# A transformer layer on one core: the normalised rows of a pair all written by ScalarE, none by VectorE

## Chip, cores and metric

The kernel runs on one core of a Trainium2 chip. The metric is the device time of one execution in microseconds (us). ACT is ScalarE, DVE is VectorE, PE is TensorE (PEld its weight loads), POOL is GpSimd, SP is SyncE.

## Reference

A layer in float32 on x of shape (16, 256, 128): attention with two heads of 64, then a feed-forward part with a routed low-rank term, both between norms.

```python
def _layernorm(x, axis=-1, eps=1e-05):
    m = jnp.mean(x, axis=axis, keepdims=True)
    v = jnp.var(x, axis=axis, keepdims=True)
    return (x - m) / jnp.sqrt(v + eps)
...
    # attention: q, k, v from the normalised rows, half of each head rotated, softmax, Wo
    # ffn: x @ W.T + the low-rank term of the best of 4 experts (ranks 1, 2, 4, 8), weighted
x = L0_attn_x
x = x + _layernorm(_L0_attn_ref(_layernorm(x, axis=-1), ...), axis=-1)
x = x + _layernorm(_L0_ffn_ref(_layernorm(x, axis=-1), ...), axis=-1)
return x
```

The change touches the first `_layernorm`, the one ahead of the attention.

## The kernel before

The 16 batches are taken in 8 pairs. A pair has 512 rows, which lie in SBUF (`x_all`) as four tiles of 128 partitions x 128 columns. Every engine has its own instruction list, written out by hand; inside it nothing is reordered. Engines meet only at semaphores.

All engines run the same loop over passes, `for a in PASSES`, from -1 to 9. Pass a holds the attention of pair a, the projections of pair a+1, the end of the attention and the second norm of pair a-1, the routing and the last residual of pair a-2, and at its end the first norm of pair a+2. Passes -1 to 5 have such a first norm (pairs 1 to 7); that of pair 0 is done ahead of the loop, by `normalise_first` on ACT (L291), four tiles in a row.

The first norm of pair n goes as follows. DVE takes statistics (`stats`, `gap`, `mean`, `variance`); POOL raises the variance to the power -0.5 (`norm_rows`, L201) and makes the shift (`norm_shift`, L206 and L208), which posts `rstd1`. Then the four tiles of `xn` are written as scale x + shift, tiles 0 and 1 by DVE (`normalise` with half 0, a tensor_scalar, L464) and tiles 2 and 3 by ACT (`normalise`, an activation Identity with a scale and a bias per partition, L296). Each tile adds 1 to `xn_ready`. PE waits for all four and transposes them into the bank ps_b:

```python
def turn_x(n):
    pe.wait_ge(xn_ready, 4 * n + 4)
    ...
    for t in range(PT):
        last = pe.transpose(ps_b[:, t * P:(t + 1) * P], xn[:, t, :], ident[:, :])     # L831
```

ACT copies ps_b to `xn_up` (`rows_up`, L301), DVE takes the remainder as `xn_low` (`rows_low`, L469, early in the next pass), and PE multiplies both by the projection weights (L838 to L840).

What stands around it at the end of a pass. On PE: `weigh(a, 2)` (L877 into ps_c), `project_z(a-1, 0)` (L898), `turn_x(a+2)` (L831), `project_z(a-1, 1)` (L898), `scores(a+1, 0)` (L857), `weigh(a, 3)` (L877 into ps_a). On ACT: `x2_copy` (L338), `variance_y` (L332), `qkt_copy` (L316), `normalise` (L296), `probs_copy(a, 3)` (L327), `rows_up` (L301), `v_copy` (L311). On DVE: `variance_2` (L516), `normalise` (L464), four `residual_z` (L599), `weights_sum` (L480), `scaled_bias` (L521), `add_head` (L488), `add_bias(a-1, 0)` (L527), `add_head`; then, in the next pass, `add_bias(a-2, 1)` (L527), which needs the second `project_z`, `rows_low` (L469), two small reductions and `row_max` (L475), which lets ACT go on with the exponentials (`exps`, L321) of the next pair. In passes -1 and 0 several one-off steps of `later_weights` are mixed in (L606 and L607 on DVE, L931 on PE, which waits for L630 on DVE).

Of the kernel before, what the change touches and what calls it, by code (L numbers as in the profile page):

```python
# [21 lines left out]
PT = 2 * TILES  # L22
# [21 lines left out]
def layer(nc, x, w_attn, vectors, w_ffn, w_down, sim, out):  # L44
# [3 lines left out]
    with ctx:  # L48
        def sb(name, shape, dt=F32):
            return ctx.enter_context(nc.sbuf_tensor(name, shape, dt))  # L50
# [4 lines left out]
        def sem(name):  # L55
            return ctx.enter_context(nc.semaphore(name))
# [26 lines left out]
        x_all, y_all = sb("x_all", [P, B * T]), sb("y_all", [P, PAIRS * PT, VW])  # L83
# [3 lines left out]
        ve1, mean1, rs1, nm1 = sb("ve1", [P, 2, PT]), sb("mean1", [P, 2, PT]), sb("rs1", [P, 2, PT]), sb("nm1", [P, 2, PT])  # L87
        xn, xn_up, xn_low = sb("xn", [P, PT, E]), sb("xn_up", [P, PT, P], F32R), sb("xn_low", [P, PT, P], F32R)
# [42 lines left out]
        link1, var1, pool1, rstd1 = sem("link1"), sem("var1"), sem("pool1"), sem("rstd1")  # L131
        xn_ready, xt_done, xt_out, xt_low = sem("xn_ready"), sem("xt_done"), sem("xt_out"), sem("xt_low")
# [15 lines left out]
        def has(n):  # L148
            return 0 <= n < PAIRS

        def rows(n, t):
            return slice(n * PT * E + t * E, n * PT * E + (t + 1) * E)
# [123 lines left out]
        def _(act):  # L276
# [15 lines left out]
                                   bias=nm1[:, 0, t:t + 1], scale=rs1[:, 0, t:t + 1]).then_inc(xn_ready, 1)  # L292

            def normalise(n):
                for t in (2, 3):
                    act.activation(xn[:, t, :], x_all[:, rows(n, t)], ACT.Identity,  # L296
                                   bias=nm1[:, n % 2, t:t + 1], scale=rs1[:, n % 2, t:t + 1]).then_inc(xn_ready, 1)

# [67 lines left out]
            for a in PASSES:  # L366
                now, nxt, done = has(a), has(a + 1), has(a - 2)
# [52 lines left out]
        def _(dve):  # L420
# [35 lines left out]
            def variance(n):  # L456
                dve.wait_ge(link1, n * 3 + 3)
                dve.scalar_tensor_tensor(ve1[:, n % 2, :], tmp1[:, 1, :], 1.0 / E, tmp1[:, 2, :], ALU.mult, ALU.add).then_inc(var1, 1)  # L458

            def normalise(n, half):  # L460
                if half == 0:
                    dve.wait_ge(rstd1, n + 1)
                for t in (2 * half, 2 * half + 1):
                    dve.tensor_scalar(xn[:, t, :], x_all[:, rows(n, t)], rs1[:, n % 2, t:t + 1], nm1[:, n % 2, t:t + 1],  # L464
                                      ALU.mult, ALU.add).then_inc(xn_ready, 1)

            def rows_low(n):
                dve.wait_ge(xt_out, n + 1)
                dve.tensor_tensor(xn_low[:, :, :].rearrange("p t c -> p (t c)"), ps_b[:, :],  # L469
                                  xn_up[:, :, :].rearrange("p t c -> p (t c)").bitcast(F32), ALU.subtract).then_inc(xt_low, 1)  # L470


            def row_max(n, u):
                dve.wait_ge(scores_done, n * 4 + u + 1)
                dve.tensor_reduce(neg_max[:, u, :], ps_s[u % 2][:, :].rearrange("p (j k) -> p j k", j=TILES),  # L475
                                  AX.X, ALU.max, negate=True).then_inc(max_ready, 1)
# [47 lines left out]
            def add_bias(n, k):  # L524
                dve.wait_ge(scaled, n + 1)
                dve.wait_ge(r_done, n * 2 + k + 1)
                dve.tensor_tensor(route[:, 2 * k:2 * k + 2, :], ps_z[k][:, :, 0:RW],  # L527
                                  bias_s[:, 2 * k:2 * k + 2, :], ALU.add).then_inc(route_ready, 1)
# [4 lines left out]
            def top_logit(n):  # L533
                dve.wait_ge(route_ready, n * 2 + 2)
                dve.tensor_reduce(top[:, :], route[:, :, PROJ + RANK:RW], AX.X, ALU.max).then_inc(route_link, 1)

            def square_sum(n):
                dve.wait_ge(squared, n + 1)
                dve.tensor_reduce(norm2[:, :], proj_sq[:, :, :], AX.X, ALU.add).then_inc(route_link, 1)
# [15 lines left out]
            def top_key(n):  # L555
                dve.wait_ge(route_link, n * 10 + 4)
                dve.tensor_reduce(key_top[:, :], key[:, :, :], AX.X, ALU.max).then_inc(route_link, 1)
# [143 lines left out]
            link(dve.tensor_scalar(bias_y[:, :], bias_y[:, :], mean_w[:, 3:4], None, ALU.subtract), fold_link)  # L701

            for a in PASSES:
                now, nxt, far, last_, done = has(a), has(a + 1), has(a + 2), has(a - 1), has(a - 2)
                if done:
                    add_bias(a - 2, 1)
                if nxt and a >= 0:
                    rows_low(a + 1)
                if done:
                    top_logit(a - 2)  # L710
                    square_sum(a - 2)
                if now:
                    row_max(a, 0)
                if done:
                    length(a - 2)
                if last_:
                    weights_sum(a - 1, 3)
                if done:
                    below_top(a - 2)
                if last_:  # L720
                    add_head(a - 1, 3, 0)
                    add_head(a - 1, 3, 1)
                if now:
                    row_max(a, 1)
                if a == 0:
                    later_weights(1)
                if a == 1:
                    later_weights(5)
                if done:
                    keys(a - 2)  # L730
                if has(a + 3):
                    stats(a + 3, 0)
                if done:
                    top_key(a - 2)
                    logits(a - 2)
                    is_top(a - 2)
                if has(a + 3):
                    stats(a + 3, 1)
                    stats(a + 3, 2)
                if done:  # L740
                    shares(a - 2)
                    pick(a - 2)
                if has(a + 3):
                    stats(a + 3, 3)
                if done:
                    sum_exps(a - 2)
                if last_:
                    residual_y(a - 1, 0)
                if done:
                    invert_sum(a - 2)  # L750
                if has(a + 3):
                    gap(a + 3)
                if done:
                    gates(a - 2)
                if has(a + 3):
                    mean(a + 3)
                if done:
                    gates_up(a - 2)
                if has(a + 3):
                    variance(a + 3)  # L760
                if done:
                    gates_low(a - 2)
                if now:
                    row_max(a, 2)
                if last_:
                    residual_y(a - 1, 1)
                    residual_y(a - 1, 2)
                if now:
                    row_max(a, 3)
                    weights_sum(a, 0)  # L770
                if a == 0:
                    later_weights(2)
                if last_:
                    stats_2(a - 1, 0)
                if now:
                    add_head(a, 0, 0)
                if last_:
                    stats_2(a - 1, 1)
                if now:
                    add_head(a, 0, 1)  # L780
                if last_:
                    residual_y(a - 1, 3)
                    stats_2(a - 1, 2)
                    stats_2(a - 1, 3)
                if now:
                    weights_sum(a, 1)
                if last_:
                    gap_2(a - 1)
                if now:
                    add_head(a, 1, 0)  # L790
                if last_:
                    square_2(a - 1)
                if now:
                    add_head(a, 1, 1)
                if last_:
                    variance_2(a - 1)
                if far:
                    normalise(a + 2, 0)
                if done:
                    residual_z(a - 2, 0)  # L800
                    residual_z(a - 2, 1)
                    residual_z(a - 2, 2)
                if done:
                    residual_z(a - 2, 3)
                if now:
                    weights_sum(a, 2)
                if a == -1:
                    later_weights(0)
                if a == 0:
                    later_weights(3)  # L810
                if last_:
                    scaled_bias(a - 1)
                if now:
                    add_head(a, 2, 0)
                if last_:
                    add_bias(a - 1, 0)
                if now:
                    add_head(a, 2, 1)
                if a == 0:
                    later_weights(4)  # L820
# [209 lines left out]
```

## Time and profile before

| what | value |
|---|---|
| time, median of 3 runs | 167.34 us (165.85 to 168.54) |
| time of the profiled execution | 168.68 us |
| its span, first to last instruction | 166.9 us |
| mean granted TensorE clock, as a share of full speed | 0.92 |
| PE busy | 132.7 us, 80% |
| DVE busy | 131.6 us, 79% |
| ACT busy | 112.0 us, 67% |
| POOL busy | 90.6 us, 54% |

The profile records one execution, whose time lies 1.78 us above its span and 1.34 us above the median. An engine's share of busy time is a mean over the start, the steady passes and the end, which have different limits. "Idle before" gives the time in which an engine stood still before an instruction, and the instruction that released it.

### The profile page before, as it was taken

What the parts mean: (1) busy time and instruction counts of PE and PEld (TensorE: products, weight loads), DVE (VectorE), ACT (ScalarE), POOL (GpSimd) and SP (SyncE); (2) the same over time, 40 slices, a digit from 0 to 9 for tenths busy, and PEclk for the clock granted to TensorE, in tenths of its full rate; (3) what the DMA queues carried; (4) which work ended last, traced back from release to release, by engine and by line L of the source; (5) the groups of instructions that cost most, each with busy time, mean ns of one, the idle gap of its engine ahead of it and who ended that gap; (6) DMA issues with size and microseconds to landing.
All of it is one profiled execution on the core that took longest, in us unless ns stands there. A gap on an engine that the chain in (4) does not pass through costs nothing.

```text
span 166.9 us, 3027 instructions
## 1 busy us (share of the span) xinstructions
PE 132.7 (80%) x865; PEld 108.6 (65%) x865; DVE 131.6 (79%) x560; ACT 112.0 (67%) x369; POOL 90.6 (54%) x150
## 2 busy tenths in 40 slices
PE   0468589967998999999999999999999799256030
PEld 0246267855887869887977897797889589145020
DVE  4669947586888899899979998897898889774512
ACT  3167535955979699879969996997998667240130
POOL 6272850670465586849657774976469516405202
PEclk9999957999999999999999999999999999965555
DMA  4533240000000000100010010001001000101001
GB/s 106 174 83 108 68 121 0 6 0 0 2 0 4 2 0 0 67 0 0 2 67 2 0 41 22 4 0 63 2 6 63 0 4 13 50 0 63 2 0 63
DMA packets 4912, 5.02 MB, mean 30 GB/s; under 512 B 369, under 2 KB 4640, under 8 KB 4896
## 3 DMA queue, kind: packets, MB, share of 16 engines
q1 hardware_dynamic: 4512, 4.46, 8.5%
q10 hardware_dynamic: 384, 0.38, 1.0%
q8 instruction: 7, 0.11, 0.3%
q14 instruction: 9, 0.07, 0.2%
HBM read 2.74 MB, written 2.10 MB: 29 GB/s over the span
## 4 chain that ended last, share of the span: by engine, by line
PE 46%; DVE 23%; ACT 18%; POOL 4%; DMA 3%; issue 3%; POOLq 1%; DVEq 0%; ACTq 0%
PE ps_s L857 6%; PE ps_z L898 6%; PE ps_a L877 5%; ACT probs L321 5%; PE ps_b L831 4%; DVE neg_max L475 3%; DMA x_all<-x 3%; PE ps_c L877 3%; ACT sq_y L332 3%; PE ps_a L867 2%; DVE x_all L495 2%; PE ps_z L912 2%; ACT qk_t L316 2%; PE ps_b L877 2%; ACT sq_z L355 2%
## 5 line engine op out<-in xcount | busy, mean ns | idle before, releaser
L321 ACT ACTIVATE probs<-ps_s,neg_max 128x256 f32<-128x256 f32 x64 | 27.1, 486 | 11.8 <-DVE neg_max L475 11.8
L475 DVE TENSOR_REDUCE neg_max<-ps_s 128x2 f32<-128x512 f32 x32 | 21.6, 681 | 4.0 <-PE ps_s L857 4.0
L857 PE MATMUL ps_s<-qk_t 64*128 64x256 f32 x128 | 19.2, 418 | 0.9 <-ACT probs L321 0.9
L877 PE MATMUL ps_a<-v_all,probs_t 128*128 128x129 f32 x128 | 18.0, 283 | 0.0
L217 POOL TENSOR_TENSOR turn<-qk,sin_x 128x256 f32<-128x256 f32 x16 | 11.9, 746 | 9.7 <-ACT qk L305 9.3
L877 PEld LDWEIGHTS ps_a<-v_all,probs_t 128*128 128x128 f32 x128 | 15.6, 191 | 2.3 <-issue 2.3
L228 POOL TENSOR_TENSOR inv_norm<-norm,power 128x4 f32<-128x4 f32 x8 | 8.1, 1015 | 15.0 <-DVE norm L544 15.0
L898 PE MATMUL ps_z<-w_z,x_t 128*128 128x190 f32 x64 | 14.2, 357 | 2.0 <-DVE x_all L599 2.0
L857 PEld LDWEIGHTS ps_s<-qk_t 64*128 64x128 f32 x128 | 11.9, 195 | 5.8 <-issue 5.2
L232 POOL TENSOR_TENSOR rsy<-var_y,power 128x4 f32<-128x4 f32 x8 | 8.6, 1070 | 12.6 <-ACT sq_y L332 12.6
L495 DVE SCALAR_TENSOR_TENSOR x_all<-y_all,rsy,x_all 128x128 f32<-128x128 f32 x32 | 13.7, 448 | 0.8 <-POOL rsy L232 0.8
L599 DVE SCALAR_TENSOR_TENSOR x_all<-ps_z,rsz,x_all 128x128 f32<-128x128 f32 x32 | 9.0, 342 | 6.1 <-POOL rsz L238 6.1
L898 PEld LDWEIGHTS ps_z<-w_z,x_t 128*128 128x128 f32 x64 | 11.2, 208 | 2.5 <-DVE x_all L599 2.4
L220 POOL TENSOR_TENSOR qk<-qk,cos_x 128x256 f32<-128x256 f32 x16 | 12.1, 754 | 1.3
L201 POOL TENSOR_TENSOR rs<-ve,power 128x4 f32<-128x4 f32 x8 | 8.1, 1018 | 8.0 <-DVE ve L458 8.0
L223 POOL TENSOR_TENSOR qk<-qk,turn 128x256 f32<-128x256 f32 x16 | 11.6, 726 | 1.3
L332 ACT ACTIVATE sq_y<-y_all 128x129 f32<-128x129 f32 x32 | 9.9, 325 | 2.6 <-DVE y_all L488 2.6
L242 POOL TENSOR_TENSOR std<-ve,root 128x4 f32<-128x4 f32 x8 | 8.2, 1030 | 5.7 <-DVE ve L516 5.7
L867 PE MATMUL ps_a<-ident,probs 128*128 128x128 f32 x64 | 9.7, 274 | 1.8 <-DVE y_all L488 1.8
L236 POOL TENSOR_TENSOR var_z<-var_z,eps 128x4 f32<-128x4 f32 x8 | 1.6, 204 | 17.3 <-ACT sq_z L355 17.3
L905 PE MATMUL ps_d<-ident_r,gated 128*128 128x128 f32 x8 | 2.5, 308 | 10.0 <-DVE gated L593 10.0
L327 ACT ACTIVATE probs_t<-ps_a 128x512 f32<-128x512 f32 x16 | 9.8, 614 | 0.6 <-PE ps_a L867 0.5
(205 smaller groups left out, 423.8 us busy)
## 6 DMA issues: line engine op xcount, KB each, us to landing
x_all<-x SPq DMA_DIRECT2D x8, 256.0 KB, 2.8
out<-x_all SPq DMA_DIRECT2D x7, 256.0 KB, 2.1
vec<-vectors ACTq DMA_DIRECT2D x1, 273.0 KB, 4.3
w_raw<-w_attn SPq DMA_DIRECT2D x1, 256.0 KB, 5.1
out<-x_all SPq DMA_DIRECT2D x2, 128.0 KB, 1.7
ffn_raw<-w_ffn ACTq DMA_DIRECT2D x1, 71.5 KB
down_raw<-w_down ACTq DMA_DIRECT2D x1, 23.5 KB
sim_raw<-sim ACTq DMA_DIRECT2D x1, 0.5 KB
```

What stands on the lines that cost most here:

```text
L217: pool.tensor_tensor(turn[:, b, :, :, :], swapped, sin_x[:, :, :, :, :].rearrange("p t g h i -> p (t g) h i"), ALU.mult).then_inc(rope_mid, 1)
L220: pool.tensor_tensor(spatial, spatial, cos_x[:, :, :, :, :].rearrange("p t g h i -> p (t g) (h i)"), ALU.mult).then_inc(rope_mid, 1)
L223: pool.tensor_tensor(spatial, spatial, turn[:, b, :, :, :].rearrange("p g h i -> p g (h i)"), ALU.add).then_inc(rope_done, 1)
L321: last = act.activation(probs[:, u, j, :], ps_s[u % 2][:, j * T:(j + 1) * T], ACT.Exp, bias=neg_max[:, u, j:j + 1])
L327: act.activation(probs_t[:, u, :, :], unit_bank[u][:, :].rearrange("p (a t) -> p a t", a=TILES), ACT.Copy).then_inc(pt_out, 1)
L332: last = act.activation(sq_y[:, t, :], y_all[:, n * PT + t, :], ACT.Square, scale=E ** -0.5, accum_out=var_y[:, t:t + 1])
L475: dve.tensor_reduce(neg_max[:, u, :], ps_s[u % 2][:, :].rearrange("p (j k) -> p j k", j=TILES), AX.X, ALU.max, negate=True).then_inc(max_r ...
L495: dve.scalar_tensor_tensor(x_all[:, rows(n, t)], y_all[:, n * PT + t, 0:E], rsy[:, t:t + 1], x_all[:, rows(n, t)], ALU.mult, ALU.add).then ...
L857: last = pe.matmul(ps_s[h][:, j * T:(j + 1) * T], qk_t[r, b, 0, j * P:(j + 1) * P], qk_t[r, b, 1, :], start=True, stop=True)
L867: last = pe.transpose(unit_bank[u][:, i * T + j * P:i * T + (j + 1) * P], probs[:, u, j, i * P:(i + 1) * P], ident[:, :])
L877: last = pe.matmul(unit_bank[u][:, j * VW:(j + 1) * VW], probs_t[:, u, i, j * P:(j + 1) * P], v_all[:, at:at + VW], start=(i == 0), stop=( ...
L898: last = pe.matmul(ps_z[k][:, t, :], x2_t[:, 2 * k + t, :], w_z[:, :], start=(t == 0), stop=False, skip_group_check=True)
```

## The change

In passes -1 to 5 the tiles 0 and 1 of `xn` move from DVE to ACT, so that ACT writes four tiles and DVE none. The count that PE waits for stays the same. The lines behind the removed function move up by 7, those behind the removed call by 9.

```diff
@@ scalar
             def normalise(n):
-                for t in (2, 3):
+                for t in range(PT):
                     act.activation(xn[:, t, :], x_all[:, rows(n, t)], ACT.Identity,
                                    bias=nm1[:, n % 2, t:t + 1], scale=rs1[:, n % 2, t:t + 1]).then_inc(xn_ready, 1)
@@ vector
-            def normalise(n, half):
-                if half == 0:
-                    dve.wait_ge(rstd1, n + 1)
-                for t in (2 * half, 2 * half + 1):
-                    dve.tensor_scalar(xn[:, t, :], x_all[:, rows(n, t)], rs1[:, n % 2, t:t + 1], nm1[:, n % 2, t:t + 1],
-                                      ALU.mult, ALU.add).then_inc(xn_ready, 1)
...
-                now, nxt, far, last_, done = has(a), has(a + 1), has(a + 2), has(a - 1), has(a - 2)
+                now, nxt, last_, done = has(a), has(a + 1), has(a - 1), has(a - 2)
...
-                if far:
-                    normalise(a + 2, 0)
```

On ACT at the end of pass 0, the piece of the difference of its instruction list:

```order
 L332 ACTIVATE sq_y,var_y<-y_all 128x129 x2
 L316 ACTIVATE qk_t<-ps_s 128x512
-L296 ACTIVATE xn<-x_all,nm,rs 128x128 x2
+L296 ACTIVATE xn<-x_all,nm,rs 128x128 x4
 L327 ACTIVATE probs_t<-ps_a 128x512
 L301 ACTIVATE xn_up<-ps_b 128x512
```

Two more activations stand between the copy of qk_t and that of probs_t; passes 1 to 5 read the same, and in pass -1 the four stand directly ahead of L301.

On DVE at the end of a steady pass (here pass 3), the kernel before:

```order
L516 SCALAR_TENSOR_TENSOR ve<-tmp 128x4
L464 TENSOR_SCALAR xn<-x_all,rs,nm 128x128 x2
L599 SCALAR_TENSOR_TENSOR x_all<-ps_z,rsz,x_all 128x128 x4
L480 RECIPROCAL den<-ps_c 128x2
L521 TENSOR_TENSOR bias_s<-bias_b,std 128x248
L488 SCALAR_TENSOR_TENSOR y_all<-ps_c,den,bias_y 128x128
L527 TENSOR_TENSOR route<-ps_z,bias_s 128x124
L488 SCALAR_TENSOR_TENSOR y_all<-ps_c,den,bias_y 128x128
L527 TENSOR_TENSOR route<-ps_z,bias_s 128x124
L469 TENSOR_TENSOR xn_low<-ps_b,xn_up 128x512
```

and the changed kernel at the same place:

```order
L509 SCALAR_TENSOR_TENSOR ve<-tmp 128x4
L592 SCALAR_TENSOR_TENSOR x_all<-ps_z,rsz,x_all 128x128 x4
L473 RECIPROCAL den<-ps_c 128x2
L514 TENSOR_TENSOR bias_s<-bias_b,std 128x248
L481 SCALAR_TENSOR_TENSOR y_all<-ps_c,den,bias_y 128x128
L520 TENSOR_TENSOR route<-ps_z,bias_s 128x124
L481 SCALAR_TENSOR_TENSOR y_all<-ps_c,den,bias_y 128x128
L520 TENSOR_TENSOR route<-ps_z,bias_s 128x124
L462 TENSOR_TENSOR xn_low<-ps_b,xn_up 128x512
```

The pair of tensor_scalars is gone, and the last residual follows the variance directly. The instruction list of PE keeps its order.

## Rows read from the trace of the kernel before

**Rows 1.** The page: busy time of each engine.

```profile
PE 132.7 (80%) x865; PEld 108.6 (65%) x865; DVE 131.6 (79%) x560; ACT 112.0 (67%) x369; POOL 90.6 (54%) x150
```

**Rows 2.** The chain that ended last, in order of time: start, us, what.

```profile
8.74 1.65 ACT xn L291 x4
...
52.99 0.78 ACT xn L296 x2
53.81 0.66 PE ps_b L831 x4
...
68.92 0.66 PE ps_b L831 x4
69.58 0.66 PE ps_z L898 x4
70.33 0.29 DVE route L527
70.62 0.60 DVE xn_low L469
71.53 0.61 DVE neg_max L475
```

**Rows 3.** Waits: engine and line, releaser: us in total, times, longest.

```profile
DVE route L527 <- PE ps_z L898: 5.4, 7, 1.0
...
PEld ps_b L831 <- ACT xn L296: 3.6, 6, 1.7
...
PE ps_b L831 <- ACT xn L296: 1.9, 3, 1.4
```

**Rows 4.** Timeline, end of pass 2 (67 to 71 us): start, us, engine, line.

```profile
67.99 0.88 ACT L296 ACTIVATE xn<-x_all,nm,rs 128x128 f32<-128x128 f32 x2
68.92 0.42 PEld L831 LDWEIGHTS ps_b<-ident,xn 128*128 128x128 f32 x4 [0.32 <-ACT xn L296]
69.62 0.60 ACT L301 ACTIVATE xn_up<-ps_b 128x512 fp32r<-128x512 f32 x1 [0.25 <-PE ps_b L831]
66.82 0.59 DVE L464 TENSOR_SCALAR xn<-x_all,rs,nm 128x128 f32<-128x128 f32 x2
67.33 1.11 DVE L599 SCALAR_TENSOR_TENSOR x_all<-ps_z,rsz,x_all 128x128 f32<-128x128 f32 x4
70.33 0.29 DVE L527 TENSOR_TENSOR route<-ps_z,bias_s 128x124 f32<-128x124 f32 x1 [0.62 <-PE ps_z L898]
```

**Rows 5.** Timeline, end of pass 0 (36 to 40 us).

```profile
37.48 0.87 ACT L296 ACTIVATE xn<-x_all,nm,rs 128x128 f32<-128x128 f32 x2
36.28 0.96 DVE L464 TENSOR_SCALAR xn<-x_all,rs,nm 128x128 f32<-128x128 f32 x2
38.71 0.39 PE L931 MATMUL ps_z<-sim_r,down_raw 32*128 32x15 f32 x2 [0.96 <-DVE sim_r L630]
39.26 0.66 PE L831 MATMUL ps_b<-ident,xn 128*128 128x128 f32 x4
```

**Rows 6.** Timeline, end of pass -1 (19 to 23 us).

```profile
20.66 0.86 ACT L296 ACTIVATE xn<-x_all,nm,rs 128x128 f32<-128x128 f32 x2
19.89 1.51 DVE L464 TENSOR_SCALAR xn<-x_all,rs,nm 128x128 f32<-128x128 f32 x2
21.57 1.11 PE L831 MATMUL ps_b<-ident,xn 128*128 128x128 f32 x4 [1.45 <-ACT xn L296]
19.80 0.72 POOL L217 TENSOR_TENSOR turn<-qk,sin_x 128x256 f32<-128x256 f32 x1
```

**Rows 7.** Windows: us, PE, PEld, DVE, ACT, POOL busy (instructions), PEclk, DMA share, GB/s.

```profile
20.00:21.00 1.00, 0.13 (x2) 0.00 (x0) 1.00 (x2) 0.84 (x2) 0.92 (x2) 0.85 0.39 46
21.00:22.00 1.00, 0.42 (x2) 0.43 (x3) 0.97 (x3) 0.52 (x2) 0.92 (x2) 0.50 0.63 214
...
27.50:28.00 0.50, 0.50 (x4) 0.41 (x3) 0.50 (x4) 0.50 (x2) 0.00 (x0) 0.98 0.00 0
...
34.00:36.00 2.00, 0.72 (x7) 0.51 (x6) 1.89 (x8) 0.98 (x2) 1.64 (x3) 1.00 0.00 0
```

## The prediction

> **What bounds the kernel now.** I start with the busy shares [rows 1]. PE and DVE stand at 80% and 79%, ACT at 67%, so by the shares alone the change looks like relief for a loaded engine at the cost of a freer one. A share doesn't say which wait ends last at the place of the change, so I go on to the chain that ended last. At the end of pass 1 it runs through the very instructions that are changed: the two ACT tiles of xn, then turn_x on PE [rows 2]. In pass 2 it comes down PE: turn_x, the second project_z, and then over to DVE, where add_bias (L527) is released, rows_low and row_max follow [rows 2]. The reader should see that turn_x lies ahead of the point where PE hands the work to DVE.
>
> The list of waits says how often that hand-over binds [rows 3]. PE's weight loads for turn_x waited for ACT's tiles of xn in six places, 3.6 us in all, and PE's matmuls in three of them. In none was the releaser the DVE tiles of xn. There are seven such places (passes -1 to 5); the timeline shows which one is missing, pass 0, where PE comes to turn_x late because it had waited for DVE's sim_r (L630) [rows 5]. DVE in turn stood still before L527 seven times, 5.4 us in all, each time until the second project_z on PE had ended [rows 3]. So DVE, busy as it is, waits for PE right there, and PE had just waited for ACT.
>
> The timeline of pass 2 gives the order to the hundredth [rows 4]. DVE starts its two tiles at 66.82 and is through at 67.41. ACT starts its two at 67.99 and ends at 67.99 + 0.88 = 68.87. The weight load of turn_x starts at 68.92, after an idle time of 0.32. The DVE half has been ready for 1.5 us by then. It is the ACT half that is late.
>
> **What the change adds.** ACT gets two more activations per pass. A run of two took 0.86 to 0.88 us [rows 4 to 6]; a run of four of the same kind on the same shape stands at the start of this kernel and took 1.65 [rows 2]. The two extra tiles cost 1.65 - 0.87 = 0.78 us. They can't start earlier than the old two, since ACT comes straight from the copy of qk_t, and PE needs all four. So xn is complete 0.78 later in each of the seven passes, measured from the work before it.
>
> Pass by pass, against the start of turn_x:
> - Pass -1: the tiles end at 20.66 + 0.86 = 21.52 and turn_x starts at 21.57 [rows 6]. Cover 0, cost 0.78.
> - Pass 0: they end at 37.48 + 0.87 = 38.35, turn_x starts at 39.26 [rows 5]. Cover 0.91, of which about 0.05 is the hand-over seen in the other passes. The new end is 39.13. Cost 0, with less than 0.1 to spare; if this cover were gone the cost would be 0.78.
> - Pass 1: they end at 52.99 + 0.78 = 53.77, turn_x starts at 53.81 [rows 2]. Cost 0.78.
> - Passes 2 to 5: as in pass 2 [rows 4], an end 0.05 before turn_x; the weight loads waited in each of them, since six of the seven places waited [rows 3]. Cost 0.78 each. In pass 2 PE's matmuls show no idle time there, only the weight loads, so PE had other work till about that moment; but that bounds a gain from an earlier xn, not a loss from a later one.
>
> That makes 6 x 0.78 = 4.7 us.
>
> **Does the delay pass on?** Behind the waiting turn_x on PE are queued the second project_z, scores of the next pair and the last weigh. The second project_z releases DVE's L527 (the chain shows 69.58, then 70.33), and from there rows_low, row_max and the exponentials [rows 2]. Both ways on, PE's and DVE's, start behind turn_x, and so does ACT's, which waited 0.25 us for turn_x before xn_up [rows 4]. probs_copy(a, 3) on ACT slips too, but the weigh that needs it stands behind turn_x as well. I find no piece of the next pass that is late now for another reason and could soak up the 0.78, so I take all of it. The lower end of this term is 0 for a pass in which such a piece exists, the upper end is 0.78.
>
> **What the change removes.** DVE's queue gets shorter by 67.33 - 66.82 = 0.51 us in a steady pass [rows 4], by at most 0.96 in pass 0 [rows 5] and 1.51 in pass -1 [rows 6]. The work behind it, the last residuals and the first half of add_bias, comes earlier, and then DVE meets the wait for the second project_z at L527. It waited 0.62 there in pass 2 [rows 4]; it will now wait about 0.62 + 0.51 + 0.78 = 1.9 us. The gain is hidden by that wait, so it counts as 0. If this cover were wrong, it would be worth up to 0.51 a pass. The removed wait for rstd1 on DVE costs and saves nothing: ACT waits for the same count.
>
> **A rule on the removed work.** In pass -1 the two DVE tiles took 1.51 us, with POOL's rotation running from 19.80 on [rows 6]; in pass 0 they took 0.96 [rows 5], in pass 2 0.59 [rows 4]. The Trainium skill, GPSIMD Engine Reference, section "8. Key points", says that GpSimd shares its SBUF interfaces with VectorE and contends with VectorE instructions that use both ports. By that rule the tensor_scalars are dearer than they look beside POOL, and their removal would give back 0.92 + 0.37 us more than 0.59 twice. By the rows both places lie in passes -1 and 0, ahead of a DVE wait, so the sum stays at 4.7; with the rule's relief counted in full it would be 3.4.
>
> **The sum.** The profiled execution took 168.68; I expect 168.68 + 4.7 = 173.4 for one like it. On the median of the runs shown, 1.34 lower, it is 167.34 + 4.7 = **172.0 us**, 2.8% slower. A measurement of this kernel can tell about 2%, or 3.3 us, from no change; the three runs themselves spread over 2.7 us.
>
> **The rivals.**
> - *Part of the delay is paid back by DVE.* DVE is nearly full in the steady passes, and if the shorter queue does move the point at which PE is released, each delayed pass costs 0.78 - 0.51 = 0.27, or 6 x 0.27 = 1.6: 169.0 us. Against it stands that DVE waits for PE at L527 in seven passes [rows 3], just behind the removed work.
> - *DVE is the bound after all: faster.* The place is DVE's queue from variance_2 to L527. The gain would be 5 x 0.51 + 0.96 + 1.51 = 5.0 us at most: 162.3 us. It decides from the point at which ACT has more than 0.78 us of cover before turn_x. Only pass 0 has that (0.91), and there PE waits for DVE's sim_r, behind a DVE wait for PE. The port rule above would feed this rival.
> - *The clock moves: slower still, or better than forecast.* The granted clock fell from full to half speed at about 20.9 us, after PE had been almost idle, and came back at about 27.5 [rows 7]; turn_x of pass -1 at 21.57 is in that stretch. PE ran some 5.9 us of it at 1.2 GHz in place of 2.4. A start 0.78 later could lengthen that stretch. Half as long again would add some 1.5 us (a twofold stretch at most 3): 173.5 to 175. It could as well end sooner, for 170.5. In the steady passes a new wait of 0.78 is short beside the gap of pass 0, where PE was busy 0.72 of 2.00 us and the clock stayed at 1.00 [rows 7].
> - *The change does not do what it says.* The instruction lists show it done in all seven passes; no chance.
>
> **Chances.** Forecast (six delays passed on in full): 0.64. Partly paid back: 0.15. Clock, upward: 0.10; clock, downward: 0.05. Faster: 0.04. The rest, 0.02, is what I can't name. The range must take in 169.0 and the spread of a median, and part of the upward clock case: 168.8 to 174.3. That leaves out the faster case, most of the clock case above 174.3 and some of the paid-back case. Faster by over 2% (under 164.0) has 0.04. Within 2% (to 170.7) are the paid-back case, half of the downward clock case and the part of the forecast where one or two passes are covered and the runs fall low: 0.22. Slower: 0.74.
>
> **What the changed profile would show.** L296 as runs of four, 1.65 us each; L831's weight loads idle about 1.1 us before them in passes 2 to 4, and PE's matmuls about 0.75, with ACT xn as the releaser; DVE idle before the second L527 of about 1.9 us; a steady period that grows from 15.1 (turn_x at 53.81 and 68.92 [rows 2]) to 15.9; ACT busy up by 14 activations of 0.39, or 5.5 us; DVE busy down by some 5; pass 0's turn_x released by PE's own queue. The forecast is wrong if the period stays at 15.1, if DVE's idle time at L527 grows by 0.51 only, or if the stretch of half clock near 21 us changes its length by more than a microsecond.

## The result, and the profile after

The changed kernel took 172.46 us, median of 4 runs (171.76 to 172.59), against 167.86 of the kernel before (4 runs, 165.85 to 168.54). The ratio is 1.029, 95% interval 1.024 to 1.033: slower by 2.9%. Ratios, here and below, rest on the runs that lie within 1.5% of the fastest one of their kernel, so they can differ a little from the quotient of two medians over all runs. The profiled execution took 172.59, its span is 170.8 us where it was 166.9.

The page of the changed kernel, busy time by engine, answers to [rows 1]:

```profile
PE 131.9 (77%) x865; PEld 108.1 (63%) x865; DVE 127.6 (75%) x546; ACT 117.4 (69%) x383; POOL 90.6 (53%) x150
```

ACT is busy 5.4 us more (14 more instructions), DVE 4.0 us less (14 fewer). PE, whose work did not change, fell from 80% to 77% of a longer span. The waits of the changed kernel, us in total, times, longest, answer to [rows 3]; L822 is the old L831, L520 the old L527, L473 the old L480:

```profile
DVE route L520 <- PE ps_z L889: 9.3, 7, 1.8
PEld ps_b L822 <- ACT xn L296: 8.6, 6, 2.5
...
PE ps_b L822 <- ACT xn L296: 6.9, 6, 2.2
...
DVE den L473 <- PE ps_c L868: 4.2, 7, 1.4
```

The weight loads of turn_x waited for ACT's tiles in the same six places, but for 8.6 us in place of 3.6, and the matmuls now in all six where they had in three, for 6.9 in place of 1.9: 5.0 us more by either row, 0.83 a place. DVE's wait before the second add_bias grew from 5.4 to 9.3 us. The end of pass 2 in the timeline answers to [rows 4]:

```profile
69.24 1.65 ACT L296 ACTIVATE xn<-x_all,nm,rs 128x128 f32<-128x128 f32 x4
71.63 0.60 ACT L301 ACTIVATE xn_up<-ps_b 128x512 fp32r<-128x512 f32 x1 [0.26 <-PE ps_b L822]
69.41 0.17 DVE L473 RECIPROCAL den<-ps_c 128x2 f32<-128x2 f32 x1 [0.22 <-PE ps_c L868]
69.50 0.71 DVE L514 TENSOR_TENSOR bias_s<-bias_b,std 128x248 f32<-128x248 f32 x1
72.35 0.29 DVE L520 TENSOR_TENSOR route<-ps_z,bias_s 128x124 f32<-128x124 f32 x1 [1.43 <-PE ps_z L889]
70.94 0.42 PEld L822 LDWEIGHTS ps_b<-ident,xn 128*128 128x128 f32 x4 [1.21 <-ACT xn L296]
```

ACT's run of four takes 1.65 us and ends at 70.89; turn_x starts 0.05 later, as it did before. The start of turn_x in the timelines of both kernels, by pass:

| pass | -1 | 0 | 1 | 2 | 3 | 4 | 5 |
|---|---|---|---|---|---|---|---|
| before, us | 21.57 | 39.26 | 53.81 | 68.92 | 84.04 | 99.16 | 113.94 |
| after, us | 22.47 | 39.74 | 55.06 | 70.94 | 86.82 | 102.71 | 118.25 |
| later by | 0.90 | 0.48 | 1.25 | 2.02 | 2.78 | 3.55 | 4.31 |

Each of passes 1 to 5 adds 0.76 to 0.77 us, 3.83 in all. Pass -1 comes 0.90 later, of which 0.13 was there before it (the first load of x landed later: DVE's first statistics start at 5.60 in place of 5.47). At pass 0 only 0.48 of it is left, 0.35 without the shift of the load. At the end 0.4 us comes off again. The chain before has 0.41 us of issue time ahead of one small DVE instruction, `norm<-norm,least`, and the chain after has 0.04 there. In the kernel before it reads:

```profile
156.18 0.16 DVE L544 TENSOR_TENSOR norm<-norm,least 128x4 f32<-128x4 f32 x1 [0.47 <-DVE norm L539]
```

### The profile page after: what moved, and what is told of

Its sections match the earlier page's. It is cut to its first block, busy times and chain, and to the rows that moved or that the text cites. A ratio compares the mean times of both kernels' runs of the same rounds, so it can differ in the third digit from the quotient of the medians.

```text
span 170.8 us, 3027 instructions
## 1 busy us (share of the span) xinstructions
PE 131.9 (77%) x865; PEld 108.1 (63%) x865; DVE 127.6 (75%) x546; ACT 117.4 (69%) x383; POOL 90.6 (53%) x150
## 4 chain that ended last, share of the span: by engine, by line
PE 40%; ACT 26%; DVE 22%; POOL 4%; DMA 3%; issue 2%; POOLq 1%; DVEq 0%; ACTq 0%
PE ps_s L848 6%; ACT xn L296 5%; PE ps_a L868 5%; ACT probs L321 5%; PE ps_z L889 4%; PE ps_b L822 4%; ACT sq_y L332 4%; ACT qk_t L316 3%; DVE neg_max L468 3%; DMA x_all<-x 3%; DVE x_all L488 2%; PE ps_z L903 2%; PE ps_b L868 2%; ACT sq_z L355 2%; DVE y_all L481 2%
## 5 line engine op out<-in xcount | busy, mean ns | idle before, releaser
L822 PE MATMUL ps_b<-ident,xn 128*128 128x128 f32 x32 | 6.2, 324 | 7.3 <-ACT xn L296 6.9
L520 DVE TENSOR_TENSOR route<-ps_z,bias_s 128x124 f32<-128x124 f32 x16 | 4.5, 283 | 9.4 <-PE ps_z L889 9.3
L296 ACT ACTIVATE xn<-x_all,nm,rs 128x128 f32<-128x128 f32 x28 | 11.6, 500 | 0.0
```

## The experiments

All ratios are to the kernel before, with their 95% intervals. Kernels of a group ran on the same chip, in five rounds with the kernel before, whose median was 168.11 us in the first group (the first four experiments), 167.94 in the second (the next four) and 168.11 in the third (the last three). "Distance" is the time from one turn_x on PE to the next in the trace.

**The added work alone.** Two more ACT activations, DVE's two tiles kept.

```diff
             def normalise(n):
+                for t in (0, 1):
+                    act.activation(spare[:, t, :], x_all[:, rows(n, t)], ACT.Identity,
+                                   bias=nm1[:, n % 2, t:t + 1], scale=rs1[:, n % 2, t:t + 1])
                 for t in (2, 3):
```

> This kernel keeps the two VectorE tiles of the kernel before and gives ScalarE two more activations of the same kind ahead of its own two, into a spare tile that nobody reads. It has the added work of the change without the removed work. Theory (the added ScalarE work is the whole cost, VectorE's relief is hidden by its wait for the second project_z): as slow as the changed kernel, 172.5 us or a ratio of 1.028 to the kernel before; turn_x of passes 1 to 5 comes 0.77 us later per pass, and VectorE's idle time before the second add_bias is near 1.4 us. Rival (the shorter VectorE queue paid back part of the delay in the changed kernel): slower than the changed kernel by up to 0.5 us a pass, 174 to 176 us, a ratio of 1.04 or more.

Measured: 172.99 us, 1.029 (1.026 to 1.033). In the timeline turn_x of pass 2 waits for ACT, and DVE's second add_bias for PE:

```profile
70.98 0.66 PE L835 MATMUL ps_b<-ident,xn 128*128 128x128 f32 x4 [0.79 <-ACT xn L300]
72.39 0.29 DVE L531 TENSOR_TENSOR route<-ps_z,bias_s 128x124 f32<-128x124 f32 x1 [1.38 <-PE ps_z L902]
```

turn_x stands at 55.10, 70.98, 86.85, 102.74 and 118.26, and the distances from pass 0 on are those of the changed kernel within 0.02 us. With DVE's work still there the passes are exactly as slow; in them DVE's relief paid nothing back.

**The removed work alone.** DVE's two tiles gone, nothing added; the rows of all later pairs are partly not computed.

```diff
             def turn_x(n):
-                pe.wait_ge(xn_ready, 4 * n + 4)
+                pe.wait_ge(xn_ready, 2 * n + 4)
...
-                if far:
-                    normalise(a + 2, 0)
```

> This kernel removes VectorE's two tiles and adds nothing: ScalarE writes its two, TensorE waits for two. Tiles 0 and 1 of the normalised rows then stay those of the first pair, so the rows of all later pairs are partly not computed. Theory: no change, a ratio of 0.995 to 1.005, about 167.9 us, with turn_x of passes 1 to 5 at the same times as in the kernel before and VectorE's idle time before the second add_bias longer by up to 0.5 us. Rival (VectorE bounds the steady passes, or its tiles beside GpSimd hold up more than themselves): 0.5 us a pass less, 163 to 165 us, a ratio of 0.97 to 0.985.

Measured: 167.76 us, 0.998 (0.995 to 1.001). The distances between one turn_x and the next from pass 0 on are 14.55, 15.12, 15.11, 15.12 and 14.76 us; the kernel before has 14.55, 15.11, 15.12, 15.12 and 14.78. The rival in which DVE bounds the passes is out. The way from pass -1 to pass 0, where the tensor_scalars had met POOL's rotation, took 17.48 us and lies with the other kernels in the table at the end of this section, so their removal beside POOL gained nothing there either.

I had expected up to 0.5 us more idle time before the second add_bias, and that is not what came. Over the whole run that wait stayed at 5.5 us, where it had been 5.4; the wait for the third weigh, which stands earlier in DVE's queue, grew from 1.7 us in three places to 4.3 in seven. At the end of pass 2:

```profile
67.62 0.17 DVE L473 RECIPROCAL den<-ps_c 128x2 f32<-128x2 f32 x1 [0.23 <-PE ps_c L868]
69.79 0.29 DVE L520 TENSOR_TENSOR route<-ps_z,bias_s 128x124 f32<-128x124 f32 x1 [0.66 <-PE ps_z L889]
```

**The change in passes 1 to 5 alone.**

```diff
             def normalise(n):
-                for t in (2, 3):
+                for t in (range(PT) if n >= 3 else (2, 3)):
...
-                if far:
+                if far and not (a + 2 >= 3):
```

> This kernel makes the change for pairs 3 to 7 alone (passes 1 to 5); passes -1 and 0 stay as before. Theory: five delays of 0.77 us, 3.9 us in all, a ratio of 1.023, about 171.7 us. Rival (a good part of the cost comes from the start, where the clock is at half speed): 2.5 us or less, a ratio under 1.015.

Measured: 171.39 us, 1.0195 (1.015 to 1.024). The distances are 15.33, 15.87, 15.88, 15.88 and 15.53, 0.75 to 0.78 longer than before, 3.81 in all. The ratio is under the 1.023 that I expected, which the interval still takes in, and above the rival's 1.015. The five passes carry the cost.

**The change in passes -1 and 0 alone.** The same edit with `n <= 2`.

> This kernel makes the change for pairs 1 and 2 alone (passes -1 and 0). Theory from the trace of the changed kernel: turn_x of pass -1 comes 0.78 us later, but the clock returns to full speed at the same time as before, near 28 us, so that less of TensorE's work runs at half speed and only 0.35 us is left at turn_x of pass 0; pass 0 itself is covered and costs nothing; a ratio of about 1.002. Rival 1 (the delay of pass -1 passes on in full, and 0.35 was chance): 0.78 us at turn_x of pass 0, a ratio of 1.005. Rival 2 (the half-speed stretch grows with the longer wait): 1.5 us or more, a ratio over 1.009.

Measured: 168.42 us, 1.002 (0.999 to 1.005), so the time can't tell it from nothing, nor my first two cases from each other. Its distances from pass 0 on are those of the kernel before within 0.02 us, so pass 0's cover held. What pass -1 does is told by the trace: the clock came back near 27.5 us here as it did before, though turn_x came 0.73 us later. The table below takes this up.

**The order on ACT, four tiles.** ACT's four tiles directly behind x2_copy.

```diff
+                if has(a + 2):
+                    act.wait_ge(rstd1, a + 3)
+                    normalise(a + 2)
                 if now:
                     variance_y(a, 0)
                 if nxt:
                     qkt_copy(a + 1, 0)
-                if has(a + 2):
-                    act.wait_ge(rstd1, a + 3)
-                    normalise(a + 2)
```

> The changed kernel with ScalarE's four tiles moved ahead of variance_y and of the copy of qk_t, directly behind x2_copy. ScalarE does the same work as in the changed kernel. Theory (the cost of the change is the place of the late tiles in ScalarE's queue, not the work): the tiles end near the time at which TensorE comes to turn_x by itself; what stays is at most some 0.15 us a pass, since xn_up now stands behind more work on ScalarE; a ratio to the kernel before of 1.000 to 1.008. Rival (ScalarE as a whole is now the bound, so that the order does not matter): 172 us, 1.025.

Measured: 167.89 us, 1.003 (0.999 to 1.007). ACT does all the work of the changed kernel, and the cost is gone but for 0.1 us in each of the three middle passes (distances of 15.2 where 15.1 stood); the first and the last distance are shorter than before (14.23 and 14.63 in place of 14.55 and 14.78). The rival in which ACT's load is the bound is out. At the end of pass 2:

```profile
66.66 1.64 ACT L296 ACTIVATE xn<-x_all,nm,rs 128x128 f32<-128x128 f32 x4
69.74 0.60 ACT L301 ACTIVATE xn_up<-ps_b 128x512 fp32r<-128x512 f32 x1
70.37 0.69 DVE L462 TENSOR_TENSOR xn_low<-ps_b,xn_up 128x512 fp32r<-128x512 f32 x1 [0.32 <-ACT xn_up L301]
68.36 0.66 PE L822 MATMUL ps_b<-ident,xn 128*128 128x128 f32 x4
```

The tiles end at 68.30, turn_x starts at 68.36 with no idle time before its matmuls, and the wait that is left has moved: xn_up now stands behind variance_y and the two copies, and DVE waits 0.32 for it.

**The same order, two tiles on each engine.** The edit of the last run, made to the kernel before.

> The kernel before, two tiles on each engine, with ScalarE's two moved ahead of variance_y and of the copy of qk_t. Theory: turn_x was held by ScalarE's two tiles by the 0.17 us or less that TensorE's matmuls stood idle in passes 1 to 5; with them earlier the gain is 0.1 to 0.2 us a pass and up to 0.7 us in pass -1, in all 0.5 to 1.5 us, a ratio of 0.991 to 0.998. Rival (the whole wait of the weight loads, 0.3 us or more a pass, was lost time): over 2 us, a ratio under 0.988.

Measured: 165.71 us, 0.988 (0.985 to 0.992). The gain is larger than I expected. The distances are 14.23, 14.88, 14.88, 14.87 and 14.32: 0.24 us less in the middle passes, though PE's matmuls had shown no idle time there. The weight loads had: 0.32 us [rows 4]. In this run they start before the matmuls of project_z have ended, without a wait:

```profile
67.16 0.52 PEld L831 LDWEIGHTS ps_b<-ident,xn 128*128 128x128 f32 x4
66.57 0.91 PE L898 MATMUL ps_z<-w_z,x_t 128*128 128x190 f32 x4
67.32 0.60 PE L831 MATMUL ps_b<-ident,xn 128*128 128x128 f32 x4
```

Summed over the five distances that is 74.68 - 73.18 = 1.50 us. In a middle pass every matmul between one turn_x and the next keeps its place in both traces, but for two steps: from project_z to turn_x it takes 0.75 us in place of 0.93, and from turn_x to the second project_z 0.44 in place of 0.50. So 0.24 of the 0.32 that the weight loads had shown was lost time, and the truth lies between my two cases. Another 0.60 us of this trace's gain lies in the way from pass -1 to pass 0 (17.09 us in place of 17.69); the table and the last run tell where that came from.

**All four tiles on DVE.**

```diff
-                if has(a + 2):
-                    act.wait_ge(rstd1, a + 3)
-                    normalise(a + 2)
...
-                for t in (2 * half, 2 * half + 1):
+                for t in range(PT):
```

> The mirror image: all four tiles on VectorE, none on ScalarE. Theory: in a steady pass VectorE's queue grows by 0.51 us against an idle time of 0.62 us before the second add_bias, so nothing is lost there, and turn_x no longer waits for ScalarE, a gain of 0.1 to 0.2 us a pass; in pass -1 the four tiles run beside GpSimd's rotation and take near 3 us in place of 1.5, so that turn_x comes about 1.4 us later; together a ratio of 0.995 to 1.006. Rival (the queue of VectorE is the bound): 0.5 us a pass more, a ratio of 1.015 or more.

Measured: 169.00 us, 1.006 (1.004 to 1.009), the end of my range, and for another reason than given: in pass -1 turn_x did come 1.3 us later, but I had taken the steady passes to gain. The middle distances grew from 15.1 to 15.4, half of what the rival held. DVE's idle time of 0.62 before the second add_bias was no room for 0.51 us more: the first project_z needs the bank that the last residual frees, and it was met first.

```profile
66.62 1.11 DVE L461 TENSOR_SCALAR xn<-x_all,rs,nm 128x128 f32<-128x128 f32 x4
67.64 1.12 DVE L596 SCALAR_TENSOR_TENSOR x_all<-ps_z,rsz,x_all 128x128 f32<-128x128 f32 x4
68.30 0.91 PE L895 MATMUL ps_z<-w_z,x_t 128*128 128x190 f32 x4 [0.36 <-DVE x_all L596]
```

**Four tiles early, and variance_y at the end of the pass.** Beside the edit of the early tiles, variance_y leaves its place ahead of the copy of qk_t and goes here:

```diff
                 if nxt:
                     v_copy(a + 1, 3)
+                if now:
+                    variance_y(a, 0)
```

> As the run with the four tiles moved ahead on ScalarE, and variance_y moved to the end of the pass, into ScalarE's idle time before the exponentials, since nothing needs it before the second half of it is done in the next pass. Theory: xn_up comes 0.6 us earlier than there, and the change costs nothing: a ratio of 0.992 to 1.001. Rival (ScalarE's load is the bound): 1.015 or more; a second one (variance_y at the end meets the squares of the routing, which VectorE waits for): 0.3 us a pass, 1.008.

Measured: 167.18 us, 0.993 (0.990 to 0.997). The middle distances are 14.93 to 14.98 us, under those of the kernel before, with all four tiles on ACT.

**Two tiles early, and variance_y at the end.** The edit of the last run on the split kernel.

> Two tiles on each engine, ScalarE's two directly behind x2_copy, and variance_y at the end of the pass. Theory: in the run with the two early tiles xn_up ended before VectorE asked for it, so that bringing it forward by another 0.6 us buys nothing; the same steady period of 14.9 us and a ratio of 0.985 to 0.992. Rival (ScalarE still holds TensorE up somewhere): a period under 14.8 us and a ratio under 0.983.

Measured: 166.31 us, 0.985 (0.979 to 0.992). The six runs spread from 164.22 to 167.30, so the time says little here. The trace has middle distances of 14.91 us: no gain over the run that leaves variance_y in its place (14.88), as expected.

**Idle matmuls at the start.**

```diff
+            def filler():
+                for _ in range(5):
+                    pe.matmul(ps_a[:, :], xn_up[:, 0, :], w_up[:, :], start=True, stop=True)
...
+                if a == -1:
+                    filler()
                 if nxt:
                     turn_qk(a + 1, 0, (probs_ready, 4 * a + 4) if now else (xt_low, 1))
...
+                if a == -1:
+                    filler()
                 if has(a + 2):
                     turn_x(a + 2)
```

> The kernel before, with two bursts of five idle matmuls (128x512, into a bank that nobody reads then) on TensorE in pass -1, one ahead of the first transposes of qk and one ahead of turn_x, where TensorE stands still; nothing else is changed. It tests the reading of the start: that the stretch at half clock between 21 and 28 us follows from these two gaps, and that TensorE's work in it costs half of its length. Theory: the clock stays at 1.00 from 13 us on, some 6 us of half-speed work take 3 us less, and as part of it is beside waits the gain is 1.5 to 3 us, a ratio of 0.982 to 0.991. Rival 1 (the clock falls all the same): a ratio of 1.00. Rival 2 (the work at half speed is hidden by other waits): clock at 1.00, but a ratio of 0.995 to 1.00.

Measured: 165.87 us, 0.992 (0.988 to 0.996), and the nine runs lie within 0.6 us of each other, where those of the kernel before lie 3.5 apart. The ratio is just above my range of 0.982 to 0.991; the interval reaches into it, leaves out the first rival and touches only the edge of the second (0.995). The windows (us, PE, PEld, DVE, ACT, POOL busy, PEclk, DMA share, GB/s), which answer to [rows 7]:

```profile
20.00:21.00 1.00, 1.00 (x5) 0.53 (x3) 1.00 (x2) 1.00 (x3) 0.92 (x2) 1.00 0.42 87
21.00:22.00 1.00, 0.72 (x7) 0.49 (x6) 0.95 (x3) 0.29 (x1) 0.92 (x3) 1.00 0.51 175
22.00:24.00 2.00, 2.00 (x18) 1.53 (x18) 0.94 (x2) 0.87 (x2) 0.89 (x1) 1.00 0.49 101
24.00:26.00 2.00, 2.00 (x14) 1.66 (x12) 1.97 (x8) 1.52 (x4) 0.00 (x0) 1.00 0.09 30
```

The clock stays at full speed, 2.4 GHz, where it had fallen to 1.2. The way from turn_x of pass -1 to that of pass 0 took 15.08 us; before it took 17.69.

**Early tiles and idle matmuls together.**

> Both: ScalarE's two tiles directly behind x2_copy, and the two bursts of idle matmuls. Theory: the gains add, 1.9 us of the first and 1.5 to 3 us of the second, a ratio of 0.970 to 0.980, near 164 us. Rival (the first run's gain came partly from the clock at the start, not from the steady passes): 0.980 or more.

Measured: 164.34 us, 0.981 (0.977 to 0.986), the fastest of all, 3.8 us under the median of the kernel before beside it (168.11). The sum of the two ratios' gains, 1.2% and 0.8%, is 2.0%; my range of 0.970 to 0.980 lies just beyond that, and the measured ratio is in the rival's, though the interval can't tell them apart. The traces can. With the clock at full speed the way from pass -1 to pass 0 takes 15.07 us with the early tiles and 15.08 without them, so there they gain nothing of their own. The 0.60 us that they had gained on that way without the idle matmuls belongs to the half clock, and can't be gained twice. What is left is the 1.5 us of the steady passes, and that is what the medians show: 165.87 - 164.34 = 1.53. The rival was right.

The traces of all kernels, with the stretch at half clock behind turn_x of pass -1 (from windows of a quarter microsecond) beside the length of the way to turn_x of pass 0:

| kernel | half clock after turn_x, us | way to pass 0, us |
|---|---|---|
| idle matmuls, early tiles | 0 | 15.07 |
| idle matmuls | 0 | 15.08 |
| four on DVE | 3.41 | 16.58 |
| four early, variance late | 3.41 | 16.53 |
| two early, variance late | 3.41 | 16.53 |
| two early | 4.70 | 17.09 |
| after | 5.05 | 17.27 |
| change in passes -1 and 0 | 5.17 | 17.30 |
| DVE's tiles removed | 5.46 | 17.48 |
| four early | 5.50 | 17.47 |
| before | 5.95 | 17.69 |
| added ACT work | 6.04 | 17.73 |
| change in passes 1 to 5 | 6.68 | 18.02 |

Against the 15.08 us without any, each microsecond of half clock costs 0.42 to 0.44 us of way, whatever the edit.

## Why the prediction was right

**The sum.** 172.0 was forecast, 172.46 measured; on the profiled execution 173.4 against 172.59. That the first pair agrees to 0.5 us is in part luck: between the two profiled executions the span grew by 3.9 us where the sum has 4.7, and the medians, of runs that spread over 2.7 us before, grew by 4.6. The mechanism held in its main line: ACT's late pair held turn_x, four tiles take 1.65 us, the hand-over is 0.05, in passes 1 to 5 the delay passes on in full through both PE and DVE. PE's matmuls stood idle 0.92 us before turn_x in the middle passes where I forecast 0.75, the weight loads 1.21 where I forecast 1.1.

**Passes 1 to 5.** Forecast 0.78 each, measured 0.76 to 0.77. Shown from two sides: the added work alone gives the whole cost (1.029), the removed work alone gives nothing in the distances (0.998).

**Pass 0.** Forecast 0 with less than 0.1 to spare; the tiles ended at 37.97 + 1.64 = 39.61 and turn_x started at 39.74, 0.13 later, so the cover held by the 0.08 us that it was forecast to, and turn_x was not held by ACT there in any run with the change.

**Pass -1: the term that was mis-sized.** I took 0.78 in full. turn_x did come 0.77 later, but only 0.35 was left at pass 0, since the clock came back at the same time, near 27.5 us, and less of PE's work fell into the half-speed stretch. The stretch itself is as long in both traces; the later turn_x stands further inside it. Behind turn_x lay 5.05 us of half clock in the changed kernel's trace and 5.95 in that of before, and 0.44 x 0.90 = 0.40 us is the missing part (17.69 - 17.27 = 0.42 in the table). My clock rival looked at the right place but at the wrong thing: it let the stretch grow or end sooner, and the stretch did neither. A small part of its downward price came all the same.

**The end.** The 0.4 us that came off near 156 us was in no term. It is one stretch of idle time on DVE's queue, ahead of `norm<-norm,least` of the last pair, and all thirteen traces agree on when it is there: 0.46 or 0.47 us in the six kernels that leave DVE's instruction list as it was (before, added ACT work, two early, two early with variance late, and the two with idle matmuls), none in the seven that change it, be the list shorter or longer. So it is a part of what the change does, the only gain that it brings, and it fits the 0.998 of the run that removes DVE's tiles alone. Why DVE stands still there stays open. So the terms that were off, 0.4 in pass -1 and 0.4 at the end, take the span's growth from 4.7 to 3.9 us.

**DVE's relief.** Forecast 0, hidden by the wait for the second project_z. Right as to the time in the passes, but the cover is another one. That wait was forecast to grow to 1.9 us and grew to 1.43, about the 0.78 of the delay alone; with DVE's tiles removed and nothing added it didn't grow at all. The freed 0.51 was gone before it: an earlier wait for the third weigh (L473) took 0.22, and the multiplication behind it (L514) took 0.71 in place of 0.55. POOL works beside that multiplication in both kernels; why it took longer is not shown. DVE's busy time fell by 4.0 us where I forecast some 5.

**The port rule.** The Trainium skill's rule on the shared interface (GPSIMD Engine Reference, "8. Key points") speaks of contention between GpSimd and VectorE instructions in a 2-port mode or with two SBUF inputs. The trace bears it out as far as it goes: the pair of tensor_scalars took 1.51 and 0.96 us in passes -1 and 0 and 0.59 in pass 2; that POOL was the cause was not tested. Taking them away gave no time back in those passes, since both places are ahead of a wait.

**My remark on passes 2 to 4** that PE had other work until about that moment, because its matmuls show no idle time, was too strong: the early pair gained 0.24 us a pass there.

## What to carry to other kernels

Before moving work to the engine with the lower share of busy time, look up who of the two is awaited at the join: here the fuller engine's half had been ready for 1.5 us, and what was put on the emptier one lengthened five passes of seven by its full length and one by half of it. The place in the queue counted for more than the work: with the tiles ahead of two copies that are needed later, the same load on ACT cost 0.3%, which can't be told from nothing, in place of 2.9%. And where an idle engine seems to have room, look for the first wait of others on the work that would slip, not for its own longest wait.

## What the runs showed that I had not expected

- A wait that only the weight loads show can be lost time all the same. PE's matmuls had 0 idle time before turn_x in passes 2 to 4, the weight loads 0.32 us, and taking that wait away shortened each pass by 0.24.
- The spread of the kernel before (165.87 to 169.57 in 25 runs) may come in good part from the start. The stretch at 1.2 GHz began anywhere from 19 to 23 us in the traces; it was 3.4 us long in three of them and 6.8 in the eight others that had one. Ten idle matmuls in two gaps of 1.2 and 1.45 us kept the clock at 2.4 GHz and brought nine runs within 0.6 us. That is a hint and no proof: the six runs with the added ACT work lie within 0.6 us too, without idle matmuls. The run-to-run spread is thus larger than some effects studied here, and the traces' distances from one turn_x to the next, equal within 0.02 us where the passes had the same work, told more than the times.
- One idle stretch of 0.46 us near the end of the kernel was in every trace with DVE's instruction list of before and in none with another list, and so made two kernels differ by 0.4 us far from where they had been changed.
